# Eight weight copies issued by ScalarE instead of the sync queue, and one copy of turned scores ahead of four exponentials, in a fused attention and feed-forward kernel

## What is computed

```
x = x + attn(layernorm(x))     # 16 heads of 16, rotary, mask: same 64-block, first 4 tokens, or 128 back; causal
h = silu(n @ w1.T * s1) * (n @ w2.T * s2)      # n = layernorm(x); 256 -> 1024, ternary weights
h = gelu(h @ h1.T * t1)                        # 1024 -> 1024
h = gelu(h @ h2.T * t2)                        # 1024 -> 1024
x = x + h @ w3.T * s3                          # 1024 -> 256
```

## Time and profile before

| | |
|---|---|
| median of three runs | 1086.2 us (1084.67 to 1086.23) |
| time of the profiled execution | 1084.15 us |
| its span, first to last instruction | 1082.3 us |
| mean granted clock of TensorE | 0.992 |
| busy: PE, PEld, DVE, ACT, POOL | 97%, 81%, 59%, 66%, 42% |

### The profile page before, as it was taken

One profiled execution on the slowest core, in us unless ns is written; L12 is line 12 of the kernel. 1 busy time (PEld: TensorE's weight loads), 2 busy tenths in 40 slices (PEclk: granted clock), 3 DMA queues, 4 the chain that ended last, 5 costly groups with the idle time before them and its releaser, 6 DMA issues.

```text
span 1082.3 us, 21614 instructions
## 1 busy us (share of the span) xinstructions
PE 1050.4 (97%) x7602; PEld 878.4 (81%) x7602; DVE 643.6 (59%) x1988; ACT 718.1 (66%) x1776; POOL 450.8 (42%) x622
## 2 busy tenths in 40 slices
PE   6869999999999999999999999999999999999998
PEld 3547878898788977889778897889878898889887
DVE  5865576556765568556675566655576555556322
ACT  3966676955958658667586576785676955966422
POOL 5642463433624418235263254542463431532433
PEclk9889999999999999999999999999999999999999
DMA  8788569455565356555483654736556365432540
GB/s 317 288 281 247 172 206 307 127 180 176 193 180 156 122 188 228 147 156 175 135 264 107 195 166 136 244 98 196 175 166 189 109 181 179 123 109 76 179 136 21
DMA packets 112797, 190.16 MB, mean 176 GB/s; under 512 B 7216, under 2 KB 66864, under 8 KB 111664
## 3 DMA queue, kind: packets, MB, share of 16 engines
q1 hardware_dynamic: 112256, 182.45, 54.2%
q10 hardware_dynamic: 432, 6.29, 1.4%
HBM read 150.97 MB, written 45.09 MB: 181 GB/s over the span
## 4 chain that ended last, share of the span: by engine, by line
PE 79%; ACT 9%; DVE 5%; POOL 3%; issue 2%; DMA 1%; SPq 0%; ACTq 0%; POOLq 0%; DVEq 0%
PE bank L791 35%; PE bank L761 11%; PE bank L818 5%; PE bank L562 5%; PE bank L693 5%; ACT Sm L974 4%; PE bank L629 4%; PE bank L659 3%; PE bank L667 3%; DVE Sm L1177 2%; PE bank L593 2%; ACT L994 2%; PE bank L720 1%; POOL b_lo L1469 1%; PE bank L704 1%
## 5 line engine op out<-in xcount | busy, mean ns | idle before, releaser
L974 ACT ACTIVATE Sm<-Sm,smin 128x260 f32<-128x260 f32 (+2 forms) x512 | 241.3, 473 | 154.2 <-DVE smin L1177 153.7
L791 PE MATMUL bank<-b_hi,W 128*128 128x512 f32 x512 | 209.3, 409 | 0.0
L791 PE MATMUL bank<-a_hi,W 128*128 128x512 f32 x512 | 206.5, 403 | 0.1
L791 PE MATMUL bank<-b_lo,W 128*128 128x512 f32 x512 | 201.1, 393 | 0.0
L791 PE MATMUL bank<-a_lo,W 128*128 128x512 f32 x512 | 200.8, 392 | 0.0
L761 PE MATMUL bank<-x_hi,W 128*128 128x256 f32 x512 | 125.0, 286 | 0.0
L761 PE MATMUL bank<-x_lo,W 128*128 128x256 f32 x512 | 123.4, 283 | 0.0
L1478 POOL TENSOR_TENSOR a_lo<-a_act,a_hi 128x256 fp32r<-128x256 f32 x128 | 94.4, 741 | 61.8 <-ACT a_hi L1025 61.7
L1177 DVE CUSTOM_DVE_ANT_0 Sm<-bank,msk,gmin 128x256 f32<-128x256 f32 x256 | 108.2, 478 | 9.3 <-PE bank L629 7.0
L791 PEld LDWEIGHTS bank<-a_hi,W 128*128 128x128 f32 x512 | 96.4, 188 | 17.5 <-DVE a_act L1260 0.3
L791 PEld LDWEIGHTS bank<-a_lo,W 128*128 128x128 f32 x512 | 96.5, 188 | 17.0
(11 more groups left out here) (136 smaller groups left out, 2197.7 us busy)
## 6 DMA issues: line engine op xcount, KB each, us to landing
W<-w_scratch SPq DMA_DIRECT2D x168, 512.0 KB, 4.1
qk_scratch<-split SPq DMA_DIRECT2D x56, 512.0 KB, 4.1
Qs<-qk_scratch SPq DMA_DIRECT2D x112, 128.0 KB, 4.4
Ks<-qk_scratch SPq DMA_DIRECT2D x14, 1024.0 KB, 8.9
w_scratch<-in_ffn_w SPq DMA_DIRECT2D x22, 512.0 KB, 7.0
x_in<-in_x SPq DMA_DIRECT2D x8, 512.0 KB, 7.3
stage_a<-in_ffn_w ACTq DMA_DIRECT2D x2, 2048.0 KB, 9.5
x<-in_x SPq DMA_DIRECT2D x8, 512.0 KB, 3.9
```

Of the source, the lines that this page charges most:

```text
L791: mm = nc.tensor.matmul(bank[n % 2][:, :], lhsT.bitcast(F32) if general else lhsT, rhs, start=(kk == 0 and part == 0), stop=(kk == NH - 1 ...
L974: ex = nc.scalar.activation(row, row, ACT.Exp, bias=smin[:, r, c:c + 1], scale=-1.0, accum_out=rowsum[:, i % 2, col:col + 1])
```

## The change

In the opening, SP no longer issues the eight copies of weights to `w_scratch` that stood at its step 8. ScalarE issues the same eight, with the same patterns and semaphores, at its own step 8, behind `split_hi`. In the rounds that have both attention and feed-forward work (0 to 6), ScalarE's step 8 (n == NH) does `keep_prev` of unit 6 ahead of the exponentials of unit 8 and no longer behind them. No instruction is added or dropped.

```diff
--- before.py
+++ after.py
@@ SP: beside_attention(r) @@
                     if r == -1:
-
                         if n in (9, 11, 12, 13):
                             save_split(1, n // 12, int(n in (11, 13)))
-                        if n == 8:
-                            for m in OTHERS[:EARLY]:
-                                save_weights(m)
                         if n == 12:
                             load_x(2)
@@ ScalarE: beside_attention(r) @@
                         if n == 14:
                             keep_globals(a, 0)
+                        if with_f and n == NH:
+                            keep_prev(a, n - T_LAG)
                         if n < UNITS:
                             exponentials(a, n)
...
-                        if GROUPS <= n - T_LAG < UNITS:
+                        if GROUPS <= n - T_LAG < UNITS and not (with_f and n == NH):
                             keep_prev(a, n - T_LAG)
...
                     if r == -1 and 0 <= nq - QK_STEP - 2 < 2 * NF:
                         split_hi(r, nq - QK_STEP - 2)
+                    if r == -1 and n == 8:
+
+                        for m in OTHERS[:EARLY]:
+                            src = chunk_of_weights(m)
+                            act.dma_start(w_scratch[:, m * SLOT:(m + 1) * SLOT].rearrange("p (k o) -> p k o", o=src.shape[2]),
+                                          src).then_inc(scratch_written[m], 16)
                     if r == -1 and n in LOOK_STEPS:
                         check_weights(2 + LOOK_STEPS.index(n))
```

## The result

| | before | changed |
|---|---|---|
| median of nine runs, us | 1086.23 (1083.73 to 1088.25) | 1088.77 (1087.68 to 1091.46) |
| ratio of the runs | | 1.003, 95% interval 1.0017 to 1.0043 |
| profiled execution: time, span, us | 1084.15, 1082.3 | 1089.21, 1087.2 |
| mean granted clock of TensorE | 0.992 | 0.989 |

The changed kernel is 0.3% slower. The profiled pair lies 5.1 us apart and the medians 2.5, since the profiled execution of before was a quick one. The forecast was +2.5 us and 1088 us, with 1086 to 1090 for the likeliest case.

The account below looks back on a forecast made before the run. Bounds: TensorE from 130 us; in the opening, ScalarE's wait for SP's late queries' save. 13.4 - 8.1 = +5.3, +0.4 keys' save, -3.2 copy ahead: +2.5 us on the mean 1085.3, 1088 us, range 1079 to 1091.

Parts of the forecast that it names:

- likeliest case: The forecast itself, the whole kernel 2.5 us slower, 1086 to 1090 us; chance 0.57.
- Part 1, the copy ahead: Step 9 of rounds 0 to 6: TensorE's wait for the copy to `PT_a` goes whole, 3.2 us gained.
- Part 2, the wait that goes: Opening: SP saves the first queries at about 55.6, landing by 62; ScalarE's waits go, 8.1 us given back.
- Part 2, the hold: Opening, ScalarE's step 8: its queue fills as SP's did, so ScalarE resumes at 67.2 instead of 53.81, 13.4 us later.
- Half a copy too many: Opening: six copies moved before release may be too many, so resumption was taken as 67.2 and not 67.6.
- The issues start with the split at 53.3: Opening: ScalarE's eight weight-copy issues were taken to begin at 53.3, their transfers about 1 us later.
- The first keys' save: Opening: this save slides too, landing at 78.2 while ScalarE wants the tile at 77.7; +0.4 us taken.
- The rest of the opening: From 77.47 on the chain runs over TensorE with the same instructions, so all of it shifts.
- longer case: Opening: copies and save share engines worse, or TensorE returns at half clock; another 2 to 5 us, 1091; chance 0.13.
- Fast issue: Opening: ScalarE's queue takes all eight copies without holding it, 0.7 us an issue; 1079 us, chance 0.18.
- Partial hold: Opening: queue takes three or four copies, or the save comes later; 1.8 to 3.6 us less, about 1085; chance 0.12.
- the queries' wait is not removed: Opening: the queries' save lands later than ScalarE wants it at 74.7, needing 19 us from issue; given no chance apart.

Follow-up runs that it names:

- e8: The changed kernel run once more, unaltered, beside the kernel before: 1089.50 us, ratio 1.0030.
- e1: Kernel before with only the copy of unit 6 moved ahead of unit 8's exponentials, weight copies still on SP: 1082.08 us, ratio 0.9961.
- e5: Changed kernel, but ScalarE issues two of the eight copies, the other six on SP behind the stack loads: 1076.36 us, ratio 0.9907.
- e7: Changed kernel, but ScalarE issues the eight copies one at a time, at the end of steps 8 to 15: 1077.24 us, ratio 0.9913.
- e4: Changed kernel, but the eight copies carry the same bytes in 4 KB rows, weights not rearranged, output not the layer's: 1082.09 us, ratio 0.9964.
- e2: Changed kernel without the copy ahead, so only the eight weight copies move to ScalarE: 1093.54 us, ratio 1.0075 to the kernel before.

## Why the prediction was right, and where its terms were off

**Part 1, the copy ahead: right in place and cause.** 3.2 us were forecast, and 3.57 to 3.61 measured, in all eight profiles that have it. The term left out how TensorE comes back from a wait: 0.06 us more to the next matmul, seven times.

**Part 2, the wait that goes: right.** SP's first save goes out at 56.45 in an execution that was 0.9 us late (forecast 55.6), and ScalarE's 7.60 us are gone. That it would land by 62 was too early, it took up to 8.2 us, but ScalarE asks for the tile only at 73.5.

**Part 2, the hold: right in mechanism, too large in size.** The assumption that ScalarE's queue fills as SP's did is borne out: 5.9 copies had moved at release, 6.0 were assumed. Forecast was a resumption 13.4 us late at 67.2. Measured is an idle time of 11.39 us and a resumption at 66.19, in an execution that was 0.9 us late at step 8 already; in e8's it is 65.17, 11.4 us late. From the first issue to the resumption the forecast had 13.9 us (53.3 to 67.2), and the two profiles have 14.35 and 14.45. ("Half a copy too many" is 0.9 us by the forecast's own 1.8 us a copy; it took off 0.4.) The step that failed is "The issues start with the split at 53.3": they start at 51.84, 0.13 us after the first exponentials of step 8, 2.3 us ahead of the split. ScalarE's queue of instructions runs ahead of its arithmetic, and the first three issues were done while the engine still worked on what it had been given.

**The first keys' save: right in kind, mis-sized.** +0.4 was taken and 2.0 to 2.2 us measured. ScalarE's own way to the tile was right: 10.5 us from its resumption in the forecast, 10.4 measured (66.19 to 76.60). The save's way was too short: 11.0 us from the resumption to the landing (67.2 to 78.2), and 12.6 measured (66.19 to 78.75; 12.4 in e8's profile). Issue and landing took 4.8 us, against 5.2 assumed. What the forecast left out stands ahead of them in the chain: it went from the turn of unit 8 straight to the minima. In between are TensorE's L689 (1.06 us) and VectorE's copy of a turned unit (0.6 us from 71.06 to 71.67), and the turn ran 1.12 us and not 0.66.

**The rest of the opening was taken to shift whole, and grew.** 0.9 us in e8's profile and 2.1 in the other are added behind 83 us. The longer case had named the clock, and the two growths go with mean clocks of 0.72 and 0.63 where before has 0.86. That TensorE's longer idle time is what puts more of its chain at the lower of the two clock levels is not shown: no run changes that alone, and e1, with the opening of the kernel before, has 0.70 and 25.2 us. How much of this growth belongs to the change stays open.

By terms, on e8's profile: the exponentials of unit 9 start at 65.17, before at 53.81, which is 11.36 us later. Less 8.1 us of waits given back and with 2.0 for the new wait that is 5.3 us at the row L663 (5.2 by the marks 82.65 and 77.47). Behind it 0.9 are added and in the rounds 3.6 won: +2.5 us, as forecast with 5.7 - 3.2. That the sum agrees so well is partly luck. The hold was forecast 2.0 us too large and the gain of part 1 0.4 too small, the new wait was 1.6 too small and the growth of 0.9 was not in the sum: the misses cancel to 0.1 us. The profile, too, is of a quick execution (1086.72 us, the fastest of its eight), as is that of the kernel before. By medians both parts are larger: the second alone costs 8.1 us, with an interval of 6.3 to 10.1, and the first alone wins 4.2.

**The rivals.** Fast issue didn't come, but its price of 0.7 us an issue was near: e5 and e7 show 0.56 to 0.68 us where the queue has room. Partial hold had the queue take more copies; the hold was indeed 2.0 us shorter than forecast, but with 5.9 copies moved, from the earlier start. Of the longer hold only the lower clock is seen. That the queries' wait is not removed shows up in e4, at 4.5 us, in a kernel without the long hold; the 4.2 us of e7 are a wait for the keys' save. As for the rule of the Trainium skill (DMA: Bandwidth & Descriptors, Issuing engines are not separate DMA queues) that the time to initiate is usually small: it holds for up to three of these copies, at 0.66 to 0.96 us, and not from the fourth on, where 11.84 us are spent on five.

## What to carry to other kernels

A DMA issue is cheap until its queue is full, and then it costs the time of the transfers ahead. So count the pieces that stand in a queue, and put bulk copies of small pieces on a queue whose issuer nobody waits for, behind what somebody waits for: here SP with all fourteen at the end gained 9.3 us with the other part, where moving eight to a busy engine alone lost 8.1 us (e2). Where a busy engine must issue them, spread them out, one a step (0.9913 in e7).

A short wait of the bounding engine for a copy that stands behind unrelated work is worth looking for in every round: one reordered copy gave 3.6 us, what the waits in rounds 0 to 6 and the restarts behind them had cost.

## What the runs showed of the hardware

- With 512-byte pieces three copies of 512 KB went on ScalarE's queue at 0.66 to 1.14 us each and the fourth took 1.5 to 3.7 us; in rows of 4 KB the first four took about 0.6 us each and the next four 3.24 us together.
- DMA instructions of ScalarE were issued up to 2.3 us ahead of the arithmetic instruction that stands before them in the program (51.84, split at 54.17).
- The two 512 KB DMAs of the queries' save on SP's queue took 10.5 and 12.7 us to land beside eight copies in rows of 4 KB on ScalarE's queue (e4), and 6.9 and 8.2 us beside eight in pieces of 512 bytes; the median of such DMAs in the kernel before is 4.1 us.
- The opening scattered by 2.4 us between two profiles of the changed kernel (first matmul at 109.56 and 107.17); the rounds, between the two marks, repeat within 0.04 us over the eight profiles with part 1.
- From the row of L667 or L663 at 74 to 84 us to the first matmul of the feed-forward part the same work took 23.7 us at a mean granted clock of 0.86 over its first 12 us (before, e4, e5), 25.2 at 0.70 (e1), 24.5 at 0.72 (e8) and 25.7 at 0.63 (changed kernel).
